# Entering chunks of a graph recurrence: elder chunk first, shorter offsets, a shorter lead

## What is computed

```python
mean = jnp.mean(h_new, axis=0); var = jnp.var(h_new, axis=0)
out1 = gamma * (h_new - mean) * jax.lax.rsqrt(var + BN_EPS) + beta
x = x + out1
h = jnp.maximum(_layernorm(x, axis=-1), 0.0)
h = jnp.maximum(h @ enc_w1.T + enc_b1, 0.0) @ enc_w2.T + enc_b2
def step(h, w):                       # five times
    agg = segment_sum((h @ w)[src], dst)
    ...                               # GRU gates from agg and h
```

## Time and profile before

| what | us |
|---|---|
| median of 3 runs (4136.1 to 4143.45) | 4136.42 |
| the profiled execution | 4137.52 |
| its span | 4135.9 |
| TensorE busy in it | 3774.8 (91%) |
| VectorE | 3061.5 (74%) |
| ScalarE | 2479.4 (60%) |
| GpSimd | 1381.2 (33%) |

### The profile page before, as it was taken

How to read it: one execution, slowest core, us unless ns; L and a number is a source line. 1 busy time by engine, 2 the same in 40 slices (tenths; PEclk the granted TensorE clock), 3 DMA queues, 4 the chain that set the end, 5 groups by cost and what they waited for, 6 DMA issues and landing times.

```text
span 4135.9 us, 59814 instructions
## 1 busy us (share of the span) xinstructions
PE 3774.8 (91%) x17331; PEld 2948.2 (71%) x17331; DVE 3061.5 (74%) x5526; ACT 2479.4 (60%) x4705; POOL 1381.2 (33%) x2017
## 2 busy tenths in 40 slices
PE   0128889999999999999899999999999999999999
PEld 0116578888888644555588888888888888887887
DVE  9989956577677677887668767766866876786685
ACT  1118756656656787787565655565565565566655
POOL 0021135533545320000362343244244234456624
PEclk9999999999999999999899999999999999999999
DMA  2019964544543322222143344344444334433444
GB/s 63 0 52 381 364 224 125 141 130 124 144 128 107 95 69 76 70 66 56 46 114 107 107 130 120 108 125 122 111 120 122 110 104 130 119 97 108 114 133 135
DMA packets 234209, 496.24 MB, mean 120 GB/s; under 512 B 32579, under 2 KB 100924, under 8 KB 227223
## 3 DMA queue, kind: packets, MB, share of 16 engines
q1 hardware_dynamic: 213084, 432.93, 36.6%
q0 software_dynamic: 7856, 53.36, 3.6%
q10 hardware_dynamic: 12938, 6.05, 0.7%
HBM read 409.83 MB, written 43.87 MB: 110 GB/s over the span
## 4 chain that ended last, share of the span: by engine, by line
PE 50%; issue 0%; DVE 0%; POOL 0%; ACT 0%; ACTq 0%; POOLq 0%; DVEq 0%
PE ps L2170 40%; PE ps L2288 3%; PE ps L2289 3%; PE ps L2291 1%; PE ps L2290 1%; PE ps L2332 1%; PE ps L2313 0%; PE ps L2318 0%; PE ps L2274 0%; PE ps L2202 0%; PE ps L2208 0%; PE ps L2193 0%; ACT wide L2017 0%; PE ps L2185 0%; POOL inv L2072 0%
## 5 line engine op out<-in xcount | busy, mean ns | idle before, releaser
L2170 PE MATMUL ps<-wide,hi 128*128 128x512 f32 (+2 forms) x5537 | 2139.0, 389 | 26.2 <-issue 11.0
L2170 PE MATMUL ps<-wide,lo 128*128 128x512 f32 (+2 forms) x5537 | 2078.2, 379 | 0.0
L2017 DVE CAST wide<-ring 128x1536 fp32r<-128x1536 uint8 (+2 forms) x1274 | 1311.1, 1029 | 560.8 <-PE ps L2170 555.1
L2170 PEld LDWEIGHTS ps<-wide,hi 128*128 128x128 f32 x5537 | 1043.0, 188 | 230.8 <-issue 32.9
L2170 PEld LDWEIGHTS ps<-wide,lo 128*128 128x128 f32 x5537 | 1044.8, 189 | 186.1
L2017 ACT CAST wide<-ring 128x768 fp32r<-128x768 uint8 (+1 forms) x1274 | 1153.1, 905 | 4.3 <-DMA ring<-count 3.0
L2384 ACT CAST hi<-high 128x128 fp32r<-128x128 f32 x1274 | 381.6, 300 | 991.5 <-PE ps L2170 616.2
L2109 POOL TENSOR_TENSOR lo<-hN,high 128x128 fp32r<-128x128 f32 x686 | 567.7, 831 | 757.9 <-PE ps L2170 469.2
L2109 POOL TENSOR_TENSOR lo<-hB,high 128x128 fp32r<-128x128 f32 x588 | 497.5, 847 | 763.3 <-PE ps L2170 543.9
L2166 PE MATMUL ps<-hN,hB 128*128 128x512 f32 (+1 forms) x1274 | 525.3, 569 | 5.6 <-DVE aggT L2347 4.2
L2377 ACT ACTIVATE hN<-aggT,source_scores 128x512 f32<-128x512 f32 (+1 forms) x637 | 428.8, 695 | 118.1 <-PE ps L2166 86.9
(11 more groups left out here) (247 smaller groups left out, 3498.5 us busy)
## 6 DMA issues: line engine op xcount, KB each, us to landing
ring<-count SPq DMA_DIRECT2D x490, 320.0 KB, 2.9
ring<-count SPq DMA_DIRECT2D x441, 256.0 KB, 2.6
ring<-count SPq DMA_DIRECT2D x490, 224.0 KB, 2.5
wide<-count POOLq DMA_DIRECT2D x49, 1024.0 KB, 5.7
count<-aggT SPq DMA_DIRECT2D x49, 800.0 KB, 5.1
xN<-in_x ACTq DMA_DIRECT2D x1, 2744.0 KB
out<-xN SPq DMA_DIRECT2D x1, 1064.0 KB
out<-xN SPq DMA_DIRECT2D x1, 896.0 KB
```

The costliest lines, as they stand in the source:

```text
L2017: return copy(wide[:, g % WIDE_SLOTS, c0:c1].rearrange("p (t u f) -> p t u f", u=2, f=P), rows[:, g % row_slots, c0:c1].rearrange("p (t f ...
L2170: ins = e.matmul(ps[:, c, 0:size], part[:, g % CUT_SLOTS, :], wide[:, g % WIDE_SLOTS, w0:w0 + size], start=k == 0 and part is hi, stop=k = ...
```

## The change

HEAD goes from 4 to 2 and the offsets of ENTER shrink (source from 12 to 7), so the lead is 9 steps and five chunks have `at` below 0. On TensorE, ACT and DVE the entering operations of a step stand in the reverse order, the eldest chunk's first. The waits that keep writes and reads of one bank apart are set anew: encoded waits for code of its own chunk, coded for entered of the chunk before, turned for plain of the second chunk before (third before). The combined weights are made at the steps that COMBINED_AT names, their copies one step behind. kept stands one step behind product. POOL's block has no line changed; root's offset is 1 (was 3) and added's 1 (was 2).

```diff
--- before.py
+++ after.py
@@ -65,14 +65,15 @@
 STEP_ROW_SLOTS = 6
 WIDE_SLOTS = 3
 CUT_SLOTS = 3
-HEAD = 4
+HEAD = 2
 TAKE_AT = 1
 LAG = 4
 CHAIN = {"hidden": 5, "decoded": 7, "relu": 8, "biased": 10, "opened": 11, "scaled": 12, "kept": 14, "bias": 17}
 STORE_AT = 15
 LEAVE = {"first": 0, "relu": 3, "second": 4, "shift": 7, "seen": 7, "root": 8, "even": 11, "turned": 12, "state": 15, "message": 16, "score": 17,
          "sent": 19, "scored": 20}
-ENTER = {"normal": 0, "turned": 0, "added": 2, "root": 3, "even": 5, "back": 5, "plain": 7, "coded": 7, "code": 9, "encoded": 10, "entered": 12, "source": 12}
+ENTER = {"normal": 0, "turned": 0, "added": 1, "root": 1, "even": 4, "back": 4, "plain": 5, "coded": 5, "code": 6, "encoded": 6, "entered": 7, "source": 7}
+COMBINED_AT = [0, 1, 2, 3, 8]
 EVERY = 4
 LEAVE_EVERY = [4, 3, 3]
 ATTEND_PARTS = [1, 0, 2]
@@ -1985,8 +1986,7 @@
 
             def combined_at(g):
 
-                n, odd = divmod(g - self.head[2].at, 2) if self.enter is not None else (0, 1)
-                return [n] if not odd and 0 <= n < self.enter.steps else []
+                return [n for n, at in enumerate(COMBINED_AT) if self.enter is not None and g == self.head[0].at + at]
 
             def gates_of(c):
 
@@ -2175,38 +2175,34 @@
                         if not weighing:
                             ins.then_inc(s["used"], 1)
 
+                    for c in self.entering_at(g - ENTER["encoded"]):
+                        e.wait_ge(s["code"], c.made)
+                        e.matmul(ps[:, 6, PAIR:PAIR + c.size], self.enter.dense[1][0], mid[c.made % 2][:, 0:c.size], start=True, stop=True)\
+                            .then_inc(s["encoded"], 1)
+                    for c in self.entering_at(g - ENTER["coded"]):
+                        e.wait_ge(s["plain"], c.made)
+                        if c.made > 1:
+                            e.wait_ge(s["entered"], c.made - 1)
+                        e.matmul(ps[:, 6, 0:c.size], self.enter.dense[0][0], room[2][c.made % 2][:, 0:c.size], start=True, stop=True)\
+                            .then_inc(s["coded"], 1)
+                    for c in self.entering_at(g - ENTER["back"]):
+                        e.wait_ge(s["even"], c.made)
+                        if c.made > 1:
+                            e.wait_ge(s["plain"], c.made - 1)
+                        e.wait_ge(s["added"], min(c.made + 1, len(self.head)))
+                        for b in range(c.blocks):
+                            ins = e.transpose(ps[:, 5, PAIR + b * P:PAIR + (b + 1) * P], room[1][c.made % 2][:, b * P:(b + 1) * P],
+                                              net.ident[:, :])
+                        ins.then_inc(s["back"], 1)
                     for c in self.entering_at(g - ENTER["turned"]):
                         e.wait_ge(s["normal"], c.made)
                         if c.made > 1:
                             e.wait_ge(s["added"], c.made - 1)
-                        if c.made > 3:
-                            e.wait_ge(s["plain"], c.made - 3)
+                        if c.made > 2:
+                            e.wait_ge(s["plain"], c.made - 2)
                         for b in range(c.blocks):
                             ins = e.transpose(ps[:, 5, b * P:(b + 1) * P], room[0][c.made % 2][:, b * P:(b + 1) * P], net.ident[:, :])
                         ins.then_inc(s["turned"], 1)
-                    for c in self.entering_at(g - ENTER["back"]):
-                        e.wait_ge(s["even"], c.made)
-                        if c.made > 1:
-                            e.wait_ge(s["plain"], c.made - 1)
-                        e.wait_ge(s["added"], min(c.made + 2, len(self.head)))
-                        for b in range(c.blocks):
-                            ins = e.transpose(ps[:, 5, PAIR + b * P:PAIR + (b + 1) * P], room[1][c.made % 2][:, b * P:(b + 1) * P],
-                                              net.ident[:, :])
-                        ins.then_inc(s["back"], 1)
-                    for c in self.entering_at(g - ENTER["coded"]):
-                        e.wait_ge(s["plain"], c.made)
-                        if c.made > 1:
-                            e.wait_ge(s["code"], c.made - 1)
-                        if c.made > 2:
-                            e.wait_ge(s["entered"], c.made - 2)
-                        e.matmul(ps[:, 6, 0:c.size], self.enter.dense[0][0], room[2][c.made % 2][:, 0:c.size], start=True, stop=True)\
-                            .then_inc(s["coded"], 1)
-                    for c in self.entering_at(g - ENTER["encoded"]):
-                        e.wait_ge(s["code"], min(c.made + 1, len(self.head)))
-                        if c.made > 1:
-                            e.wait_ge(s["entered"], c.made - 1)
-                        e.matmul(ps[:, 6, PAIR:PAIR + c.size], self.enter.dense[1][0], mid[c.made % 2][:, 0:c.size], start=True, stop=True)\
-                            .then_inc(s["encoded"], 1)
 
                     for c in self.due(g - LEAVE["first"], "leave"):
                         dve, _ = self.taken(c.third, MOST_BANKS)
@@ -2359,7 +2355,7 @@
                         n1 = min(n + 4, self.enter.steps)
                         e.copy(turned_w[:, n * D:n1 * D], ps[:, 2 + n // 4, 0:(n1 - n) * D]).then_inc(s["w_cut"], 1)
                 for g in self.steps:
-                    for n in combined_at(g - WIDE_SLOTS):
+                    for n in combined_at(g - 1):
                         e.wait_ge(s["w_made"], n + 1)
                         e.copy(combined[:, n, :, :].rearrange("p g f -> p (g f)"), ps[:, n, 0:3 * D]).then_inc(s["w_kept"], 1)
                     if plain <= g < total:
@@ -2425,27 +2421,27 @@
                             e.wait_ge(s["second"], c.turn)
                             e.activation(net.hT[:, c.cols], ps[:, 1 if c.lane else 6, 0:c.size], func, scale=scale, bias=bias)\
                                 .then_inc(s["next"], 1)
+                    for c in self.entering_at(g - ENTER["entered"]):
+                        _, func, _, bias = self.enter.dense[1]
+                        e.wait_ge(s["encoded"], c.made)
+                        e.activation(net.hT[:, c.cols], ps[:, 6, PAIR:PAIR + c.size], func, bias=bias).then_inc(s["entered"], 1)
+                    for c in self.entering_at(g - ENTER["code"]):
+                        _, func, _, bias = self.enter.dense[0]
+                        e.wait_ge(s["coded"], c.made)
+                        if c.made > 2:
+                            e.wait_ge(s["encoded"], c.made - 2)
+                        e.activation(mid[c.made % 2][:, 0:c.size], ps[:, 6, 0:c.size], func, bias=bias).then_inc(s["code"], 1)
+                    for c in self.entering_at(g - ENTER["plain"]):
+                        e.wait_ge(s["back"], c.made)
+                        if c.made > 2:
+                            e.wait_ge(s["coded"], c.made - 2)
+                        e.activation(room[2][c.made % 2][:, 0:c.size], ps[:, 5, PAIR:PAIR + c.size], ACT.Relu).then_inc(s["plain"], 1)
                     for c in self.entering_at(g - ENTER["normal"]):
                         e.wait_ge(s["factors"], 1)
                         if c.made > 2:
                             e.wait_ge(s["turned"], c.made - 2)
                         e.activation(room[0][c.made % 2][:, 0:c.size], net.hT[:, c.cols], ACT.Identity, scale=bn[:, 5:6],
                                      bias=bn[:, 7:8]).then_inc(s["normal"], 1)
-                    for c in self.entering_at(g - ENTER["plain"]):
-                        e.wait_ge(s["back"], c.made)
-                        if c.made > 2:
-                            e.wait_ge(s["coded"], c.made - 2)
-                        e.activation(room[2][c.made % 2][:, 0:c.size], ps[:, 5, PAIR:PAIR + c.size], ACT.Relu).then_inc(s["plain"], 1)
-                    for c in self.entering_at(g - ENTER["code"]):
-                        _, func, _, bias = self.enter.dense[0]
-                        e.wait_ge(s["coded"], c.made)
-                        if c.made > 2:
-                            e.wait_ge(s["encoded"], c.made - 2)
-                        e.activation(mid[c.made % 2][:, 0:c.size], ps[:, 6, 0:c.size], func, bias=bias).then_inc(s["code"], 1)
-                    for c in self.entering_at(g - ENTER["entered"]):
-                        _, func, _, bias = self.enter.dense[1]
-                        e.wait_ge(s["encoded"], c.made)
-                        e.activation(net.hT[:, c.cols], ps[:, 6, PAIR:PAIR + c.size], func, bias=bias).then_inc(s["entered"], 1)
                     for c in self.due(g - LEAVE["relu"], "leave"):
                         _, func, scale, bias = layers[c.layer].first
                         e.wait_ge(s["lv_first"], c.late)
@@ -2559,6 +2555,10 @@
                             else:
                                 e.tensor_tensor(h, h, new, ALU.add).then_inc(ch.sem, ch.up()); e.wait_ge(ch.sem, ch.n)
```

(8 more changed lines are left out.)

## The result

The changed kernel takes 4294.55 us (median of 4 runs, 4289.14 to 4296.9) against 4137.25 us for the kernel before (median of 4): a ratio of 1.038, 95% interval 1.0365 to 1.0395. It is 157 us slower, on the side and close to the size that was forecast (4304, +167).

The account below looks back on a forecast made before the run. TensorE, busy 91% of the span, was taken as the bound. First sums at 2038.4, step 1 at 2050.5, 19 periods of 14.4 us and the tail gave +167.4 us on 4137.52, so 4304 us; range 4250 to 4350.

Parts of the forecast that it names:

- The step that decided: Recurrence's first 40 steps: for 20 chunks the next step's sums wait for the whole chain, 5.6 us, through root and lo.
- Rival C: Recurrence: the chain does not gate, only turned waits for plain, 1.3 us more each period; 4160 us; 3%.
- D: Rival: neither wait costs anything, only the shorter prologue is seen; 4134 us, or 4128 with moved work free; 2% and 1%.
- Rival A: Recurrence: the chain gates but TensorE's clock stays at 2.4 GHz in the sums; 4264 us, +128; 15%.
- The signs: Up to 2330: 20 gaps of about 5 us ended by lo, TensorE busy below 70%, granted clock 0.6 to 0.85.
- First sums: Prologue's end: first sums start at 2038.4, 5.2 us earlier than before; bounds 2035.6 and 2042.
- The period: Two steps of the recurrence with one entering chunk: 14.4 us, 12.45 at full clock, against 5.91 before.
- chain: From the start of turned through statistics, root (3.2 us) and lo to the sums: 5.6 us.
- step 0 to 1: Recurrence's start at the low clock: sums of step 1 follow first sums by 4.19 + 2.3 + 5.6, at 2050.5.
- the tail: Steps 40 to 45: last chunks leave ten small TensorE operations of 0.25 us where there were four, 1.5 us.
- The clock: TensorE's clock falls in each period's pause and rises in the sums, low for 3.4 or 5.6 us.
- the 5 us at the start: Prologue: the shorter lead, 9 steps for 16, brings the first sums 5.2 us earlier.

Follow-up runs that it names:

- e1: Changed kernel with root's offset put back from 1 to 3, nothing else: 4150.51 us against 4129.83 for the kernel before.
- e5: Kernel before, old order, with added's offset 1 (was 2) and root's 1 (was 3): 4258.27 us against 4129.83.
- e3: Changed kernel with ten unused matmuls of 256 columns behind each turned of the recurrence: 4253.26 us against 4129.83 for the kernel before.
- e10: Changed kernel with HEAD 4 and kept three steps behind product, root still at 1: 4318.84 us against 4137.97 for the kernel before.
- e4: Changed kernel with root at 3, later offsets one longer, turned waiting for plain of the third chunk before: 4152.33 us against 4136.17 for the kernel before.
- e6: Kernel before with HEAD 2 and kept one step behind product, old order and offsets: 4148.71 us against 4136.17.
- e7: e4 with HEAD 4 and kept three steps behind product: 4141.32 us against 4137.97 for the kernel before.
- e8: e4 with HEAD 3 and kept two steps behind product: 4137.89 us against 4137.97 for the kernel before.
- e11: e1 with HEAD 4 and kept three steps behind product: 4160.72 us against 4137.97 for the kernel before.
- e2: Changed kernel with lo put ahead of root in POOL's steps, root still at 1: 4227.04 us against 4129.83 for the kernel before.

## Why the prediction was right

**The step that decided** was POOL's queue: root and added both due at step g+1, root ahead of lo, TensorE's odd sums behind lo. The trace shows the 20 pauses, e1 takes them away with one digit, e5 makes them in the kernel before. Rival C (only turned waits for plain) is what e1 is, and D did not occur. Rival A, full clock, is what e3 makes by force: 123 us over the kernel before there, for the 128 of the text. The signs that it named came too: between step 0 and step 40 TensorE is busy for 58% of the time, at a mean clock of 0.74.

**First sums**: 20.14 us behind the factor by the sum (2038.4 less 2018.26), 20.25 measured. That is closer than the working deserves, for two errors cancel. Chunk 5 was turned 13.8 us behind the factor (2030.52), not 15.1; and its root took from 2032.29 to 2036.48, 4.2 us for 2.6, since casts of steps 0 and 1 fell into it, where the text said that none disturbs it.

**The period**: 13.67 us for 14.4. Its terms: odd sums 3.86 (the text's case of 3.4 us at the low clock; I had gone to the middle of 3.4 and 5.6), coded and product 0.56 for 0.46, even sums 2.28 for 2.29, encoded to turned 1.52 for 1.8, chain 5.45 for 5.6 (the text's own terms add up to 5.53). Its root, sized at 3.2 us with one cast in it because kept would hold the second back, took 3.18 (2166.72 to 2169.90), and e10 shows the reason to be right: without that hold the second cast falls in. 19 periods of 0.74 us less are 14 us, as much as the whole miss in this Flow (167.4 forecast, 153.8 in the ledger). Smaller ones cancel: step 0 to 1 took 10.95 us for 12.1, the tail 4.2 more for 1.5.

**The clock**: it fell in each period as forecast, and rose once the sums ran. Which of the two lengths of slow sums it takes could not be had from the rows of before: the changed kernel has the shorter, e5 the longer. What sets it was not tried, and the text's middle between the two was no reading of it.

**A term left out.** The text let kept go from three steps behind product to one without a price. e4, e6, e7 and e8 show one: 0.8 us a period, on DVE's queue, whenever nothing else gates. In the changed kernel it is hidden under the pause, and by e10 it even saves something there. It is seen only past the last pause: steps 40 to 48 took 4.2 us more where the text had 1.5. Steps 40 and 42 took 3.64 us each, and the pure steps behind them 2.53 and 2.39 for 2.19 and 2.17; with kept three steps away (e11) the eight steps took 19.5 us for 22.7.

**A term that was right for the sum and wrong in its meaning**: the 5 us at the start. e8 shows that a shorter lead gives nothing back even without the two waits: 5.5 of the 7.5 us come back as work between the sums, where the text's rivals C and D had put 2.7 on it, and 2.0 as small waits.

## What to carry to other kernels

An offset in a hand-written software pipeline is a distance between two queues: before shortening one, list what stands behind the waiting operation in its queue and who needs that in the same step. Here root's offset of 1 put a chain of 5.5 us in front of lo, with nothing over it, though no line of POOL's code was changed. And when the engine that bounds the kernel is full behind a prologue, work taken out of the prologue is for the most part moved, not saved (e8). That it would pay where it lands on an engine with room was not tried here.

## What the runs showed of the hardware beyond expectation

A pause of 3.12 us in a period of 10.15 left TensorE's clock at 2.4 GHz behind fifteen of twenty pauses of e2, where one of 5.04 us in 13.67 dropped it each time. 200 extra matmuls whose results nobody reads made the stretch up to step 48 31 us shorter: the clock was 1.00 for 0.74, and the chain as long as before. And one engine's operation depends on where the other's cast falls: POOL's power took 0.71 us alone and 1.73 beside DVE's cast of 1536 bytes a row, its smallest operations 0.20 and up to 1.12.
